# Edge lists sorted by matmul ranks, payload routed within sets and scattered in runs of four

## The chip, the cores and the metric

The kernel runs on one core of one Trainium2 chip. The metric is the device time of one execution in microseconds. The core has five engines with their own instruction queues: TensorE (PE), VectorE (DVE), ScalarE (ACT), GpSimd (POOL) and SyncE (SP). DMAs are issued from SP, ACT and POOL; indirect DMAs, which take a row number per partition from a column of a tile, only from POOL.

## The reference, cut

The program is two graph layers, each followed by a mixture of experts, on 6250 nodes of 256 features. Three edge lists appear in it: `src` for sums of edge attributes, `dst` (both 106250 edges) for two attention layers with one head, and `L1_ffn_edge_index[1]` (131072 edges) for an attention with four heads.

```python
time_feat = relu(edge_attr @ W_time.T + b_time)
sums = segment_sum(time_feat, src, num_segments=n)            # list 0
...
e = leaky_relu(el[src] + er[dst], 0.2)                        # list 1, twice
ex = exp(e - segment_max(e, dst, num_segments=n)[dst])
out = segment_sum(hp[src] * (ex / segment_sum(ex, dst)[dst])[:, None], dst)
...
agg = segment_sum(h[src] * alpha[:, :, None], dst, num_segments=M)   # list 2, four heads
```

## The kernel before

Nodes lie in 49 blocks of 128 (`NB`). Each list is sorted by node block: an edge's place in the sorted list is the start of its block plus its rank in the block, and blocks begin at multiples of a group of `KS[g]` x 128 edges, so that each group belongs to one block. `sorts` computes the places of the three lists one after the other on VectorE. The keys lie on 128 partitions in 832 (lists 0, 1) or 1024 (list 2) columns. For each block L368 counts its edges in a partition, TensorE sums the counts over partitions (L331), and then for each block L353 makes a mask, L354 a running count along the row and L358 copies the count into `posf` where the mask is set. List 0's places are made for the first `EARLY` columns and then for the rest, so that POOL may begin: for each of 832 columns it scatters 128 attribute rows of 33 numbers into `attr_sorted` (L274). SP loads these rows in chunks of 16 columns (`chunk`), each when a chunk four earlier has landed. ScalarE writes the node's place in the rows (L322). X (6.4 MB) is loaded near the beginning, and VectorE ends `sorts` with the statistics of X.

For lists 1 and 2 VectorE writes a payload of four words per edge (`pay`: the other node, the node's number in its block, and its bits as bytes, L409 to L415). POOL scatters it to `pay_sorted` column by column, 128 rows of 16 bytes an instruction (`scatter_pool`, L436): 832 and 1024 instructions, dealt out by hand over the stages that follow (the `scatter=` arguments in `program`). A stage is a block of its own: it ends when all engines are through with it, its scatters included.

The stages in order are sorts, edge_sums, norm_T, adapter, ln_stats, norm_T, router0, gates, experts, ln_stats, twice gat_tables and attention, finish, ln_stats, norm_T, router_tables, attention with four heads, and last_experts. The two attentions read `pay_sorted` in 16 parts (`PART` groups each) and POOL gathers a table row per edge, 128 per instruction (L770): 464 groups of 2 gathers for list 1, 304 groups of 4 for list 2. `NGS` holds the numbers of groups.

## Time and profile before

| | us |
|---|---|
| median of 3 runs | 8061.0 (8035.8 to 8073.2) |
| the profiled execution | 8044.4 |
| its span | 8042.6 |
| POOL busy | 5679.7 (71%) |
| VectorE busy | 5366.6 (67%) |
| TensorE busy | 4395.7 (55%) |
| ScalarE busy | 3591.1 (45%) |
| DMA, mean | 53 GB/s, 427 MB |

POOL's busy time doesn't hold the issue time between two of its DMAs, which the profile shows as idle time ended by "issue". The profile's chain of waits covers only the last stage (from 7825 us on), so the order of the stages before is read from the timeline of each engine.

### The profile page before, as it was taken

The page shows a single profiled execution, that of the slowest core. Times are in us where ns is not written, and L with a number is a line of the kernel's source. Part 1 is how long each engine was busy: PE and PEld are TensorE (multiplying, and loading weights), DVE is VectorE, ACT ScalarE, POOL GpSimd, SP SyncE. Part 2 cuts the span into 40 slices and gives each one's busy share as a digit, 9 for nine tenths or more (in the row PEclk, how much of TensorE's full clock was granted, in tenths as well). Part 3 has the DMA queues.
Part 4 walks back from the last instruction along what each step waited for, and adds up shares of the span by engine and source line. Part 5 has one row for each costly group of instructions (what it writes and reads, how often), then busy time and mean ns, then how long its engine had stood idle before and what let it go on. Part 6 is the DMA issues. An engine that isn't in the chain of part 4 may idle for free. (4 is left out here: it accounts for less than half of the span.)

```text
span 8042.6 us, 111241 instructions
## 1 busy us (share of the span) xinstructions
PE 4395.7 (55%) x22490; PEld 2790.5 (35%) x22610; DVE 5366.6 (67%) x18776; ACT 3591.1 (45%) x11436; POOL 5679.7 (71%) x5781
## 2 busy tenths in 40 slices
PE   0000007914269993566666656666612777777768
PEld 0000006912135552344444434444411344444435
DVE  9999407913212223677777767777741999999987
ACT  0000003411112221477777457777710788888862
POOL 2777777777677777777777777777766777777750
PEclk9999999956689996799999889999956899999989
DMA  6111111200010000244434234433301111111113
GB/s 162 26 24 26 24 24 41 52 4 3 3 29 2 2 2 14 76 107 108 108 107 107 71 91 108 108 107 107 107 10 29 23 27 28 27 27 28 27 32 118
DMA packets 476333, 427.34 MB, mean 53 GB/s; under 512 B 269726, under 2 KB 409876, under 8 KB 475668
## 3 DMA queue, kind: packets, MB, share of 16 engines
q0 software_dynamic: 214016, 282.62, 15.3%
q1 hardware_dynamic: 224020, 120.13, 5.6%
q10 hardware_dynamic: 37632, 17.48, 1.0%
q8 instruction: 203, 3.33, 0.2%
q14 instruction: 462, 3.78, 0.2%
HBM read 341.50 MB, written 78.72 MB: 52 GB/s over the span
## 5 line engine op out<-in xcount | busy, mean ns | idle before, releaser
L436 POOL DMA_INDIRECT pay_sorted<-pay,pos x1856 | 1889.8, 1018 | 697.8 <-issue 572.1
L770 POOL DMA_INDIRECT G<-tab_gat,pay x1856 | 1789.6, 964 | 592.4 <-issue 557.5
L770 POOL DMA_INDIRECT G<-tab_rt,pay x1216 | 1154.9, 950 | 433.8 <-issue 298.5
L274 POOL DMA_INDIRECT attr_sorted<-rows,pos x832 | 842.8, 1013 | 389.5 <-issue 253.3
L844 PE MATMUL pU<-G,PM 128*128 128x257 f32 x3712 | 1001.9, 394 | 1.1 <-DVE acc L1157 1.0
L790 PE MATMUL pA<-identb,G 128*20 128x128 bf16 (+1 forms) x3072 | 389.6, 226 | 933.9 <-DMA G<-tab_gat,pay 813.3
L889 ACT ACTIVATE aT<-pA 20x256 bf16<-20x256 bf16 (+1 forms) x1232 | 520.2, 422 | 517.2 <-PE pA L790 508.6
L1060 DVE TENSOR_REDUCE mt<-pW 128x4 f32<-128x2048 f32 x304 | 694.1, 2283 | 15.2 <-PE pW L808 13.8
L844 PEld LDWEIGHTS pU<-G,PM 128*128 128x128 f32 x3712 | 658.3, 198 | 58.1 <-ACT PM L941 1.2
L790 PEld LDWEIGHTS pA<-identb,G 128*20 128x20 bf16 (+1 forms) x3072 | 164.1, 92 | 1444.5 <-DMA G<-tab_gat,pay 1181.4
L322 ACT ACTIVATE rows<-lo 128x16 f32<-128x16 f32 x52 | 11.6, 229 | 1140.0 <-DMA attr_sorted<-rows,pos 1080.3
L935 ACT ACTIVATE e<-pW,adst 128x256 f32<-128x256 f32 x928 | 432.7, 466 | 165.4 <-DVE mt L1033 116.5
L1033 DVE TENSOR_REDUCE mt<-pW 128x1 f32<-128x256 f32 x928 | 389.7, 420 | 140.3 <-PE pW L800 126.6
L1649 DVE TENSOR_TENSOR t<-pO,BL 128x1024 f32<-128x1024 f32 (+1 forms) x78 | 90.7, 1163 | 580.4 <-PE pO L1601 580.3
L1633 ACT ACTIVATE H<-pH,B 128x512 f32<-128x512 f32 (+1 forms) x312 | 206.6, 663 | 591.0 <-PE pH L1590 590.1
L950 ACT ACTIVATE PT<-e,bias 128x256 f32<-128x256 f32 x928 | 456.8, 492 | 0.6 <-DVE e L1149 0.5
L1157 DVE SCALAR_TENSOR_TENSOR acc<-acc,alpha,pU 128x257 f32 x928 | 440.9, 475 | 7.8 <-PE pU L844 6.9
L1149 DVE SCALAR_TENSOR_TENSOR e<-e 128x256 f32<-128x256 f32 x928 | 398.0, 429 | 37.1 <-ACT e L935 2.7
L916 ACT ACTIVATE Nm<-iota,pay 128x128 bf16<-128x128 f32 x1216 | 383.2, 385 | 0.0
L816 PE MATMUL pP<-ident,PT 128*128 128x128 f32 x1856 | 369.6, 282 | 0.0
L335 PE MATMUL turned<-ident,gsum 128*1 128x128 f32 x24 | 5.6, 411 | 628.7 <-DVE gsum L404 628.7
L941 ACT ACTIVATE PM<-pP 128x256 f32<-128x256 f32 x928 | 334.2, 360 | 10.3 <-PE pP L816 9.1
(325 smaller groups left out, 11388.4 us busy)
## 6 DMA issues: line engine op xcount, KB each, us to landing
pay_sorted<-pay,pos POOLq DMA_INDIRECT x1856, 2.1
G<-tab_gat,pay POOLq DMA_INDIRECT x1856
G<-tab_rt,pay POOLq DMA_INDIRECT x1216, 2.4
expert_parts<-pos SPq DMA_DIRECT2D x144, 128.0 KB, 1.7
yl<-expert_parts SPq DMA_DIRECT2D x36, 512.0 KB, 3.8
attr_sorted<-zattr SPq DMA_DIRECT2D x1, 16896.0 KB, 53.5
rows<-attr_sorted ACTq DMA_DIRECT2D x256, 66.0 KB
attr_sorted<-rows,pos POOLq DMA_INDIRECT x832, 2.2
```

Of the source, the lines that this page charges most:

```text
L274: pool.indirect_dma_start(out=self.attr_sorted, out_offset=bass.IndirectOffsetOnAxis(ap=pos0[:, t:t + 1], axis=0), in_=rows[:, j, k, :], i ...
L436: pool.indirect_dma_start(out=out, out_offset=bass.IndirectOffsetOnAxis(ap=self.pos[g][:, lo + n:lo + n + 1], axis=0), in_=self.pay[g][:, ...
L770: pool.indirect_dma_start(out=G[:, j, k, 0:R], out_offset=None, in_=table, in_offset=bass.IndirectOffsetOnAxis(ap=pay[:, g % (2 * PART), k ...
L790: ins = nc.tensor.transpose(pA[j % len(pA)][:, k * P:(k + 1) * P], parts[:, k, 0:ROWS], self.identb[:, :])
L844: ins = nc.tensor.matmul(u[:, 0:F], PM[:, j % 2, k * P:(k + 1) * P], G[:, j, k, 0:F], start=(k == 0), stop=(k == K - 1))
L889: a.activation(aT[0:ROWS, j % 2, :], pA[j % len(pA)][:, 0:K * P], ACT.Copy).then_inc(s_aT, 1)
L935: a.activation(e[:, j % 2, :], pW[j % 2][:, 0:K * P], ACT.Identity, bias=ad).then_inc(s_y, 1)
L950: a.activation(PT[:, s, :], e[:, s, :], ACT.Exp, bias=bias[:, j % 4:j % 4 + 1]).then_inc(s_PT, 1)
L1033: v.tensor_reduce(mt, pW[s][:, 0:K * P], AX.X, ALU.max).then_inc(s_max, 1)
L1060: v.tensor_reduce(mt, pW[:, :, :], AX.X, ALU.max).then_inc(s_max, 1)
L1149: v.scalar_tensor_tensor(e[:, j % 2, :], e[:, j % 2, :], SLOPE, e[:, j % 2, :], ALU.mult, ALU.max).then_inc(s_e, 1)
L1157: v.scalar_tensor_tensor(ac, ac, alpha[:, j, 0:1], pU[j % 2][:, 0:F], ALU.mult, ALU.add).then_inc(s_acc, 1)
```

## The change

Ranks. VectorE only makes the masks (four buffers in turn). TensorE counts them by products with a column of ones, 128 columns of the list at a time, and sums ranks in PSUM by three kinds of products: the mask with a lower triangle (edges of earlier partitions), the counts of earlier columns, and the start of the block. VectorE copies the sums by the mask. `EARLY` goes from 208 to 256.

Payload. Lists 1 and 2 are cut into sets of 64 columns (13 and 16 sets). Within a set edges are sorted by block, each block rounded up to four edges (`CH`), into 128 x 17 chunks of four. Each half set of 32 columns is routed by 32 products: R is one-hot in the target partition, V holds three values (two parts of the other node's number, and the node's number) one-hot in the target column. R, Q and V are made by VectorE (tensor_tensor on bf16) in X's memory, so X is loaded after the last routing product. The sums of two half sets are kept (`keep`), and the payload words are built from them. `destinations` works out each chunk's row in `pay_sorted` (POOL's index), whose rows are now four edges, 64 bytes. POOL scatters 13 x 17 + 16 x 17 = 493 columns of chunks, within edge_sums, the first norm_T, the adapter and experts.

Around it. `NGS[1]` goes from 464 to 470 and `NGS[2]` from 304 to 309, since every block is rounded up in every set. The attention with one head reads `pay_sorted` as "(s p k)", that with four heads still as "(p s k)". Some small tiles of the last stages lie in the payload's memory.

```diff
 AR = 4
-EARLY = 208
...
+SC = 64
+CH = 4
+SETS = (None, ET // SC, FT // SC)
+MC = 17
+SLOTS = MC * CH
+NGS = (NG0,) + tuple((e + NB * (CH - 1) * n + NB * (k * P - CH)) // (k * P) for e, k, n in zip((E0, E1), KS[1:], SETS[1:]))
...
-        self.pay = [None, kp("pay1", [P, ET, PW], I32), kp("pay2", [P, FT, PW], I32)]
+        self.pos = [None] + [kp(f"pos{g}", [P, n], I32) for g, n in ((1, 4 * NB * NX1), (2, FT))]
...
         self.attr_sorted = nc.dram_tensor("attr_sorted", (NG0 * GE, ED + 1), F32).ap()
...
+        self.pay_sorted = [None] + [nc.dram_tensor(f"pay_sorted{g}", (NGS[g] * KS[g] * P // CH, CH * PW), I32).ap()
+                                    for g in (1, 2)]
         self.tab_gat = nc.dram_tensor("tab_gat", (PADROW + PADS, D + 3), F32).ap()
...
+            T8, HT = 8, 32
...
+            spare = self.X[:, 0:NB - 1, :].rearrange("p b d -> p (b d)").bitcast(BF16)
+            RN, VN = HT * P, 3 * SLOTS * HT
+            R = [spare[:, n * RN:(n + 1) * RN].rearrange("p (a r b) -> p a r b", a=HT // T8, b=T8) for n in range(2)]
+            V = [spare[:, 2 * RN + n * VN:2 * RN + (n + 1) * VN].rearrange("p (w a c b) -> p w a c b", w=3, a=HT // T8, b=T8)
+                 for n in range(2)]
+            Q = spare[:, 2 * RN + 2 * VN:2 * RN + 2 * VN + VN // 3].rearrange("p (a c b) -> p a c b", a=HT // T8, b=T8)
...
+            HALVES = (0, SETS[1] * SC // HT, FT // HT)
...
+                sp.wait_ge(s_routed, HALVES[1] + HALVES[2])
+                filled += self.load_x(sp)
...
+                def counts(g):
+                    for b in range(NB):
+                        n = masks[0]
+                        pe.wait_ge(s_mask, n + 1)
+                        for j in range(pairs(g)):
+                            ins = t.matmul(ptot[:, j * NB + b:j * NB + b + 1], mask[n % 4][:, j * P:(j + 1) * P], onesb[:, 0:1],
+                                           start=True, stop=True)
+                        ins.then_inc(s_used, 1)
+                        masks[0] += 1
...
+                def ranks(g, lo, to):
+                    for b in range(NB):
+                        n, u = masks[0], sels[0]
+                        pe.wait_ge(s_mask, n + 1)
+                        if u >= 2:
+                            pe.wait_ge(s_sel, u - 1)
+                        r = rank[u % 2]
+                        for a in range(lo, to, 512):
+                            z = min(a + 512, to)
+                            t.matmul(r[:, a - lo:z - lo], tris[0][:, :], mask[n % 4][:, a:z], start=True, stop=False)
+                        for a in range(lo, to, P):
+                            z = min(a + P, to)
+                            t.matmul(r[:, a - lo:z - lo], tot[:, a // P, b:b + 1].to_broadcast([P, P]), tris[min(g, 1)][:, 0:z - a],
+                                     start=False, stop=False)
+                        for a in range(lo, to, 512):
+                            z = min(a + 512, to)
+                            ins = t.matmul(r[:, a - lo:z - lo], off[0:96, b:b + 1].to_broadcast([96, P]), places_of(g)[0:96, a:z],
+                                           start=False, stop=True)
+                        ins.then_inc(s_used, 1)
+                        masks[0] += 1
+                        sels[0] += 1
...
+                def route(g):
+                    for h in range(HALVES[g]):
+                        n = halves[0]
+                        s, first_set = h // 2, HALVES[1] // 2 * (g - 1)
+                        pe.wait_ge(s_rv, n + 1)
+                        if h % 2 == 0 and first_set + s >= 2:
+                            pe.wait_ge(s_kept, first_set + s - 1)
+                        for k in range(HT):
+                            ins = t.matmul(routed[(first_set + s) % 2][:, 0:3 * SLOTS].rearrange("p (w c) -> p w c", w=3),
+                                           R[n % 2][:, k // T8, :, k % T8], V[n % 2][:, :, k // T8, :, k % T8],
+                                           start=(h % 2 == 0 and k == 0), stop=(h % 2 == 1 and k == HT - 1))
+                        ins.then_inc(s_routed, 1)
+                        halves[0] += 1
...
+                def make_mask(lo, to, b):
+                    n = masks[0]
+                    if n >= 4:
+                        dve.wait_ge(s_used, n - 3)
+                    v.tensor_scalar(mask[n % 4][:, lo:to], hi[:, lo:to], self.iota[:, b:b + 1], None, ALU.is_equal).then_inc(s_mask, 1)
+                    masks[0] += 1
...
-                        c(v.tensor_scalar(mm, hh, self.iota[:, b:b + 1], None, ALU.is_equal))
-                        c(v.tensor_tensor_scan(rk, mm, none[:, lo:hi_], base[:, b:b + 1], ALU.add, ALU.add))
-                        if keep:
-                            v.tensor_scalar(base[:, b:b + 1], rank[:, hi_ - 1:hi_], 0.0, None, ALU.add)
-                        c(v.copy_predicated(posf[:, lo:hi_], mm.bitcast(U16), rk))
...
+                def ranks(g, lo, to):
+                    def select(b):
+                        dve.wait_ge(s_used, first_mask + b + 1)
+                        v.copy_predicated(posf[:, lo:to], mask[(first_mask + b) % 4][:, lo:to].bitcast(U16), rank[sels[0] % 2][:, 0:to - lo])\
+                            .then_inc(s_sel, 1)
+                        sels[0] += 1
+                        dve.wait_ge(s_sel, sels[0])
+                    first_mask = masks[0]
+                    make_mask(lo, to, 0)
+                    for b in range(NB):
+                        if b + 1 < NB:
+                            make_mask(lo, to, b + 1)
+                        select(b)
...
+                def destinations(g):
+                    dve.wait_ge(s_iota, 5)
+                    dve.wait_ge(s_rep, g)
+                    n = SETS[g]
+                    for q in range(0, n, 5):
+                        w = min(5, n - q)
+                        both = rank[q // 10][:, q // 5 % 2 * 512:q // 5 % 2 * 512 + w * 2 * (NB + 1)]\
+                            .rearrange("p (s q b) -> p s q b", q=2, b=NB + 1)
+                        c(v.tensor_tensor(below[:, 0:w, :, :], chunk[:, :].unsqueeze(1).unsqueeze(3).to_broadcast([P, w, MC, NB + 1]),
+                                          both[:, :, 0, :].unsqueeze(2).to_broadcast([P, w, MC, NB + 1]), ALU.is_ge))
+                        c(v.tensor_tensor(below[:, 0:w, :, :], below[:, 0:w, :, :],
+                                          both[:, :, 1, :].unsqueeze(2).to_broadcast([P, w, MC, NB + 1]), ALU.mult))
+                        c(v.tensor_reduce(dsum[:, q:q + w, :], below[:, 0:w, :, :], AX.X, ALU.add))
+                    dve.sem_inc(s_repd, 1)
+                    to = self.pos[g][:, 0:n * MC]
+                    c(v.tensor_tensor(to.rearrange("p (s m) -> p s m", m=MC), dsum[:, 0:n, :],
...
+                def route(g):
+                    w, n_sets = width(g), SETS[g]
+                    kk = key[:, g, 0:w]
+                    src = key[:, 0, 0:w] if g == 1 else oth[:, :]
+                    m2, m3, f = mi[:, 0:w], mj[:, 0:w], posf[:, 0:w]
+                    c(v.tensor_copy(m2, f))
+                    c(v.tensor_scalar(m3, m2, 2, P - 1, ALU.logical_shift_right, ALU.bitwise_and))
+                    c(v.tensor_copy(rb[:, 0:w], m3))
+                    c(v.tensor_scalar(m3, m2, 9, 2, ALU.logical_shift_right, ALU.logical_shift_left))
+                    c(v.tensor_scalar(m2, m2, CH - 1, None, ALU.bitwise_and))
+                    c(v.tensor_tensor(cb[:, 0:w], m2, m3, ALU.add))
...
+                    def keep(s):
+                        first_set = HALVES[1] // 2 * (g - 1)
+                        dve.wait_ge(s_routed, HALVES[1] * (g - 1) + 2 * s + 2)
+                        v.tensor_copy(stage[:, s, :, :].rearrange("p w c -> p (w c)"), routed[(first_set + s) % 2][:, 0:3 * SLOTS])\
+                            .then_inc(s_kept, 1)
+                    for h in range(HALVES[g]):
+                        n = halves[0]
+                        if n >= 2:
+                            dve.wait_ge(s_routed, n - 1)
+                        def over(x, wide):
+                            return x[:, h * HT:(h + 1) * HT].rearrange("p (a b) -> p a b", b=T8).unsqueeze(2)\
+                                .to_broadcast([P, HT // T8, wide, T8])
+                        v.tensor_tensor(R[n % 2][:, :, :, :], places_r[:, :, :].unsqueeze(1).to_broadcast([P, HT // T8, P, T8]),
+                                        over(rb, P), ALU.is_equal)
+                        c(v.tensor_tensor(Q[:, :, :, :], places_c[:, :, :].unsqueeze(1).to_broadcast([P, HT // T8, SLOTS, T8]),
+                                          over(cb, SLOTS), ALU.is_equal))
+                        for q in range(3):
+                            ins = v.tensor_tensor(V[n % 2][:, q, :, :, :], Q[:, :, :, :], over(vals[:, q, :], SLOTS), ALU.mult)
+                        c(ins)
+                        dve.sem_inc(s_rv, 1)
+                        halves[0] += 1
+                        if h % 2 == 0 and h:
+                            keep(h // 2 - 1)
+                    keep(n_sets - 1)
...
-        PART = NG // 16
-        pay = sb("pay", [P, 2 * PART, K, PW], I32)
+        PART = -(-NG // 16)
+        if one:
+            pay = sb("pay", [P, 2 * PART, K, PW], I32)
+        else:
+            spare = self.pay[1][:, :, :].rearrange("p a b -> p (a b)")[:, 4 * K * P:4 * K * P + 2 * PART * K * PW]
...
+            rows = self.pay_sorted[gi].rearrange("n (e c) -> (n e) c", c=PW)
+            of = rows.rearrange("(s p k) c -> p s k c" if one else "(p s k) c -> p s k c", p=P, k=K)
             def load(part):
                 n = part % 2
-                sp.dma_start(pay[:, n * PART:(n + 1) * PART, :, :], of[:, part * PART:(part + 1) * PART, :, :]).then_inc(s_ld[n], 16)
+                w = min(PART, NG - part * PART)
+                sp.dma_start(pay[:, n * PART:n * PART + w, :, :], of[:, part * PART:part * PART + w, :, :]).then_inc(s_ld[n], 16)
...
-            k.edge_sums(acc0, scatter=[(1, 0, 384)])
+            k.edge_sums(acc0, scatter=[(1, 0, SETS[1] * MC), (2, 0, 60)])
             with nc.sbuf_tensor("XT0", [P, KT, NB * P], F32) as XT:
-                k.norm_T(XT, scatter=[(1, 384, 440)])
-                k.adapter(XT, acc0, scatter=[(1, 440, 588)])
-        k.ln_stats(scatter=[(1, 588, 612)])
+                k.norm_T(XT, scatter=[(2, 60, 76)])
+                k.adapter(XT, acc0, scatter=[(2, 76, 150)])
+        k.ln_stats(scatter=[])
         with nc.sbuf_tensor("XT1", [P, KT, NB * P], F32) as XT, nc.sbuf_tensor("LG0", [P, NB, NX0], F32) as LG, \
                 nc.sbuf_tensor("g0", [P, NB, NX0], F32) as g:
-            k.norm_T(XT, scatter=[(1, 612, 668)])
-            k.router0(XT, LG, scatter=[(1, 668, 724)])
-            k.gates(LG, g, NX0, True, scatter=[(1, 724, 738)])
+            k.norm_T(XT, scatter=[])
+            k.router0(XT, LG, scatter=[])
+            k.gates(LG, g, NX0, True, scatter=[])
...
                               (i["L0_ffn_expert_w2"], i["L0_ffn_expert_b2"], ACT.Relu),
-                              (i["L0_ffn_expert_w3"], i["L0_ffn_expert_b3"])], NX0, scatter=[(1, 738, ET), (2, 0, 560)])
...
-                k.gat_tables(layer, acc, m, adst, scatter=[(2, 584 + 104 * layer, 688 + 104 * layer)])
+                k.gat_tables(layer, acc, m, adst, scatter=[])
```

## Rows read from the trace of the kernel before

**Rows 1.** The page, costliest groups: count | busy, mean ns | idle before, releasers.

```profile
L436 POOL DMA_INDIRECT pay_sorted<-pay,pos x1856 | 1889.8, 1018 | 697.8 <-issue 572.1
L770 POOL DMA_INDIRECT G<-tab_gat,pay x1856 | 1789.6, 964 | 592.4 <-issue 557.5
```

**Rows 2.** Busy time by stretch; x counts instructions; last: granted clock, DMA share, GB/s.

```profile
1249.00:1769.00 520.00, 366.02 (x2816) 348.53 (x2816) 364.14 (x1795) 177.05 (x512) 391.95 (x384) 0.87 0.18 37
...
3318.70:4511.50 1192.80, 763.52 (x4177) 489.29 (x4177) 937.42 (x3751) 862.06 (x3250) 894.86 (x928) 0.97 0.40 106
...
6215.20:7797.00 1581.80, 1156.29 (x6717) 633.78 (x6838) 1468.85 (x6343) 1266.88 (x3710) 1154.95 (x1216) 0.94 0.17 29
```

**Rows 3.** POOL's timeline: start, us, instruction, in brackets idle time and its releaser.

```profile
140.24 1.14 POOL L274 DMA_INDIRECT attr_sorted<-rows,pos  x1 [136.21 <-DVE pos L388]
...
1234.10 0.97 POOL L274 DMA_INDIRECT attr_sorted<-rows,pos  x1 [0.31 <-issue]
1235.38 0.97 POOL L274 DMA_INDIRECT attr_sorted<-rows,pos  x1 [0.30 <-issue]
...
1761.54 0.97 POOL L436 DMA_INDIRECT pay_sorted<-pay,pos  x1 [0.30 <-issue]
```

**Rows 4.** VectorE's timeline, first instruction of a stage; in brackets the idle time.

```profile
1769.47 2.72 DVE L1242 TENSOR_SCALAR xn<-X,mean,rstd 128x256 f32<-128x256 f32 x8 [139.52 <-PEq L126]
...
1848.23 0.20 DVE L1313 TENSOR_SCALAR rc<-acc 128x49 f32<-128x49 f32 x1 [60.92 <-PEq L126]
...
2057.45 15.78 DVE L449 BATCH_NORM_STATS2 st<-X 128x6 f32<-128x256 f32 x48 [34.02 <-PEq L126]
...
2092.57 2.71 DVE L1242 TENSOR_SCALAR xn<-X,mean,rstd 128x256 f32<-128x256 f32 x8 [16.46 <-PEq L126]
...
2250.06 0.17 DVE L1498 TENSOR_SCALAR r<-iota 128x6 f32<-128x6 f32 x1 [27.26 <-PEq L126]
...
3133.56 15.78 DVE L449 BATCH_NORM_STATS2 st<-X 128x6 f32<-128x256 f32 x48 [74.53 <-PEq L126]
...
3318.72 0.15 DVE L996 CAST rown<-rowid 128x1 int32<-128x1 f32 x1 [33.98 <-PEq L126]
...
5859.12 0.47 DVE L1833 RECIPROCAL rd<-acc 128x49 f32<-128x49 f32 x1 [2.04 <-PEq L126]
...
5982.66 15.78 DVE L449 BATCH_NORM_STATS2 st<-X 128x6 f32<-128x256 f32 x48 [87.65 <-PEq L126]
...
6215.20 0.15 DVE L996 CAST rown<-rowid 128x1 int32<-128x1 f32 x1 [56.96 <-PEq L126]
```

**Rows 5.** Groups by shape, VectorE in sorts, list 2.

```profile
L354 DVE TENSOR_TENSOR_SCAN rank<-mask,base,none 128x1024 f32<-128x1024 bf16 x49 | 115.4, 2354 | 1.8
L358 DVE COPY_PREDICATED posf<-mask,rank 128x1024 f32<-128x1024 uint16 x49 | 63.2, 1291 | 1.7
L353 DVE TENSOR_SCALAR mask<-hi,iota 128x1024 bf16<-128x1024 bf16 x49 | 24.1, 491 | 1.7
```

**Rows 6.** Timelines of VectorE and POOL in experts and in finish.

```profile
2333.92 1.67 DVE L1656 SCALAR_TENSOR_TENSOR X<-t,g,X 128x256 f32<-128x256 f32 x4
...
2334.18 1.07 POOL L436 DMA_INDIRECT pay_sorted<-pay,pos  x1 [0.31 <-issue]
...
5865.49 17.12 POOL L436 DMA_INDIRECT pay_sorted<-pay,pos  x1 [0.30 <-issue]
...
5881.79 13.22 DVE L1845 TENSOR_TENSOR X<-X,acc 128x12544 f32<-128x12544 f32 x1
...
5882.91 12.96 POOL L436 DMA_INDIRECT pay_sorted<-pay,pos  x1 [0.30 <-issue]
```

**Rows 7.** Weight loads of TensorE in the attention with four heads.

```profile
6802.91 0.18 PEld L847 LDWEIGHTS pLU<-pfs,pay 128*128 128x128 bf16 x4
```

**Rows 8.** DMA issues: count, KB each, median us to landing.

```profile
tab_rt<-rows SPq DMA_DIRECT2D x1, 735.0 KB, 17.5
...
B<-in_L_ffn_expert_b_dram SPq DMA_DIRECT2D x2, 6.0 KB, 5.4
```

326 lines of the change are left out of this document (240 added, 86 removed).

## The prediction

> **What bounds the kernel now.** I read the costliest groups first [rows 1]: three kinds of indirect DMA on GpSimd (POOL) lead the list, and their idle time is almost all "issue", the engine's own 0.30 us between two of them. Next the stretches by stage [rows 2]: in edge_sums no compute engine fills its 520 us, and in the first attention POOL issues 928 gathers in 1193 us. Then POOL's own timeline [rows 3]: from 140 us on it issues one indirect DMA per 1.278 us (1234.10 to 1235.38) with nothing but stage boundaries between. Last, VectorE's first instruction of each stage [rows 4]: the bracket is the time since its last one of the stage before, in which only scatters were running. Where no scatter stands in front of a boundary (the start of finish, 5859.12) that is 2.04 us. So POOL's queue sets the end from 140 us to the start of the last stage, and each scatter removed is worth its 1.28 us until the stage's compute becomes the longer.
>
> **What is removed.** 1856 payload scatters become 13x17 + 16x17 = 493 (sets times MC). They now stand in edge_sums (281), the first norm_T (16), the adapter (74) and experts (122); the other stages have none. Stage by stage, against the compute that is left:
>
> edge_sums: 384 scatters filled the stage from its start at 1249 to 1762.5 [rows 2, 3], 1.337 us each; 281 take 375 us, with the 7 us from the last issue to the next stage (1762.5 to 1769.47) and a wait between the two lists of about 3 us that is 386 us. VectorE's end, 139.5 us before 1769.47, lies 381 us after the start, so POOL still ends it, by little: 520 - 386 = 134 us saved. First norm_T: 78.8 us from 1769.47 to 1848.23; 16 scatters and the 7 us leave 28, saved 51. Adapter: 34.0 - 2 = 32 [rows 4]. Three ln_stats: 16.46 - 2 = 14.4 each, 43 (the other two are alike). Two further norm_T: 60.9 less 2 for the last transposes and copies (an estimate) and 2 for the boundary, 57 each, 114. router0: 27.3 - 2 = 25; gates some 8 (an estimate: 14 scatters and a tail against its own chain). experts: 74.5 - 2 = 72. Two gat_tables: 34.0 - 2 = 32, and some 28 for the second, which is alike. finish: 87.65 - 2 = 86. router_tables: 57.0, of which the store of its table keeps 17 (17.5 us to landing [rows 8], issued 2.5 us before VectorE ends, then the boundary): 40. Sum: 666 us.
>
> **What is added outside the sorts.** Rounding each node block up to four edges per set makes more groups: NGS goes from 464 to 470 and from 304 to 309. Two layers of 6 groups of 2 gathers, 24 x 1.265 us (busy plus issue over 1856 [rows 1]) = 30 us. The router's attention takes 1581.8 us for 304 groups [rows 2], 5.2 each: 5 groups, 26 us. In attention for one head the payload is now read as "(s p k)", 3840 pieces of 32 bytes per part in place of 128 long ones. The nearest row is a bias load that I count as 1536 pieces of 4 bytes and that lands in 5.4 us [rows 8]; in proportion 13.5 us, against some 2 now (an estimate). Later parts are asked for 14 groups ahead (36 us), so only the first load of each layer shows: 2 x 11 = 22 us; bounds 0 and 50. Together 78 us. A scatter row of 64 bytes in place of 16 I cost at nothing: gathers of about 1 KB issue at the same 0.96 us [rows 1].
>
> **The sorts.** They end with POOL, not with VectorE: first scatter 140.24, last 1235.38, 832 x 1.278 = 1063 us of issue and 33 us lost. Three things move.
>
> (a) The start. VectorE's steps to the first 256 columns: preamble to 9.7 us (about 30 small operations instead of four), key split 1.3, 49 count masks, 0.49 us at 1024 columns [rows 5] so about 0.46 at 896, each waiting for seven TensorE products; four weight loads of bf16 take 0.18 us [rows 7], so seven take 0.3 and I allow 0.55 per block, 27 us. Base chain 6, lo0 and fill 2, then 49 rank steps of mask and predicated copy. The scan, 2.354 us at 1024 columns, is gone [rows 5]; at 256 columns mask and copy are about 0.3 + 0.43 and a hand-over to TensorE, 0.85 us, 42 us. Sum 89, so POOL starts 51 us earlier (bounds 75 and 115).
>
> (b) VectorE's own end. Ranks for 1024 columns cost 0.49 + 1.29 + 0.1 = 1.9 us per block instead of 4.2; TensorE's 12 products there carry 3072 columns, about 1.3 us at 2.4 GHz and 2.6 at 1.2, so either way near VectorE's pace. My sum: list 0 done at 158, list 1's ranks, chunk destinations and value preparation at 332, its routing 195, its words 27, list 2's ranks at 748, routing 240, words 31: about 1020 us. The load of X, now behind the routing, is issued when chunk 47 of 52 has been scattered, 84 us before POOL ends; load and statistics (some 60 us) fit under it. So VectorE doesn't set the end unless it loses 200 us more.
>
> (c) The routing blocks POOL. This is the term that decides. The one-hot tables R, Q and V are made by tensor_tensor with both inputs in SBUF. The row X<-X,acc in finish is such an operation, 13.22 us long, and the scatter issued under it took 12.96 us instead of 0.97 [rows 6]: it waited for the operation's end. Shorter ones let it in between: under a burst of four (1.67 us) a scatter took 1.07, it got in at the next instruction [rows 6]. The Trainium skill (SBUF — State Buffer, SBUF: two separate sides) has a VectorE operation with two SBUF inputs hold a port pair for its whole length against a GpSimd operation that reads SBUF; the first pair of rows agrees, and by its word alone scatters pass only between instructions.
>
> Length of one half set: R has 4096 elements, Q and the three of V 2176 each. The f32 row gives 1.054 ns an element (13.22 us over 12544). No row has two bf16 inputs; the bound below is the bf16 mask, 0.27 ns a column. I take half the f32 price, since all operands are bf16 in runs of 8: 2.3 + 4 x 1.3 = 7.5 us, and 14.5 at the full price. (The Trainium skill, VectorE: DVE Perf Modes, tier table, gives tensor_tensor 1224 ns for 2048 bf16 elements against 2293 in f32; by it a half set is an estimate of 7.6 us. No row here shows it.) In a half set there are five ends of instructions, two of them followed by a wait. With one scatter per boundary and 1.278 us between two, four pass per half set: POOL loses 58 x (7.5 - 4 x 1.278) = 139 us. Bounds: five or more pass and nothing is lost; only the two waits let one through, 58 x (7.5 - 2.56) = 287.
>
> About 10 us more go to the new integer preparation. The sorts change by -51 + 139 + 10 = +98 us.
>
> **Sum.** The profiled execution took 8044.4 us (span 8042.6), 17 below the median of 8061. 8044 - 666 + 78 + 98 = 7554; I say 7555.
>
> **The rivals.** (1) Nothing is blocked by bf16 pairs: 7555 - 139 = 7416. For it: only f32 rows show blocking. Against it: what blocks looks like the second input, not the type. (2) Scatters pass only at waits: 7555 + 148 = 7703. For it: in finish a scatter issued into 45 short operations without waits waited until the last, 17.12 us [rows 6]. Against: the burst row, whose four operations are nearest to the two and three of a half set. (3) tensor_tensor runs at the f32 price: 14.5 us per half set, five pass, 58 x (14.5 - 6.4) = 470 lost, VectorE ends near 1430 and POOL still after it: 7555 + 331 = 7886. (4) The 32-byte pieces slow the gathers: if the attention's 1.27 us rose by a tenth, 2 x 119 more, 7793; against it, the DMA engines are busy 0.40 there [rows 2]. (5) Slower than before: f32 price and one scatter per half set, so that POOL loses 58 x (14.5 - 1.28) = 767 us: 7555 + 628 = 8183. It turns slower once a half set costs POOL more than 10.8 us beyond what it issues. (6) The change doesn't do what it says: the stages keep their length without scatters. Against it, rows 4 leave no other releaser.
>
> **How the numbers follow.** Forecast 0.54, (1) 0.12, (2) 0.15, (3) 0.08, (4) 0.05, (5) and (6) 0.04, the rest spread. The range 7400 to 7800 holds forecast, (1), (2) and (4) with 30 us either way for my stage estimates; (3), (5) and (6) lie outside. About 0.5% is what this kernel's measurement can tell from no change. Faster by over 0.5%: 0.94; within it 0.03; slower 0.03.
>
> **What would show it.** edge_sums near 386 us with POOL last; VectorE's brackets at about 2 us before experts, finish and the rest; first scatter near 89 us; attr scatters of 2 us and more in the routing, four to a half set; tensor_tensor of 4096 bf16 elements at 2.3 us; sorts over at about 1345 us; 940 gathers in each of the two attention layers at 1.27 us. I am wrong if VectorE, not POOL, ends the sorts, if the attention slows by its payload loads, or if the half set is twice as long.

## The result and the profile after

The kernel after takes 7510.5 us (median of 4 runs, 7502.3 to 7522.8) against 8057.2 for the kernel before (4 runs): a ratio of 0.9327, 95% interval 0.9306 to 0.9347. The forecast of 7555 was 0.6% high. The profiled execution took 7504.9 us with a span of 7503.1, so the span shrank by 539.5 us, where the prediction's terms sum to 490.

First the ends of the stages. These are VectorE's first instructions of each stage in its timeline of the kernel after; the columns are those of [rows 4]: start, us, instruction, and in brackets the idle time before it with its releaser.

```profile
1332.27 0.27 DVE L833 MEMSET wt<- 128x256 f32 x1 [55.77 <-PEq L133]
1719.11 2.08 DVE L1553 TENSOR_SCALAR xn<-X,mean,rstd 128x256 f32<-128x256 f32 x6 [3.50 <-PEq L133]
1743.61 0.20 DVE L1624 TENSOR_SCALAR rc<-acc 128x49 f32<-128x49 f32 x1 [7.24 <-DVEq L133]
1921.77 15.78 DVE L754 BATCH_NORM_STATS2 st<-X 128x6 f32<-128x256 f32 x48 [1.23 <-PEq L133]
1941.13 2.03 DVE L1553 TENSOR_SCALAR xn<-X,mean,rstd 128x256 f32<-128x256 f32 x6 [0.70 <-PEq L133]
2817.63 2.71 DVE L754 BATCH_NORM_STATS2 st<-X 128x6 f32<-128x256 f32 x8 [1.06 <-PEq L133]
2953.64 0.15 DVE L1307 CAST rown<-rowid 128x1 int32<-128x1 f32 x1 [3.43 <-PEq L133]
5498.74 0.47 DVE L2144 RECIPROCAL rd<-acc 128x49 f32<-128x49 f32 x1 [1.74 <-PEq L133]
5535.12 15.78 DVE L754 BATCH_NORM_STATS2 st<-X 128x6 f32<-128x256 f32 x48 [0.70 <-PEq L133]
5654.25 0.15 DVE L1307 CAST rown<-rowid 128x1 int32<-128x1 f32 x1 [15.24 <-PEq L133]
```

The brackets that were 16 to 140 us in [rows 4] are now 0.7 to 7 us, but for the 15.24 us ahead of the last attention, where the table's store is waited for, and the 55.77 us at the end of the sorts, where POOL still runs. The differences of neighbouring rows are the stage lengths, set beside those of [rows 4]. The sorts of the kernel before end with this row of the same timeline:

```profile
1248.79 0.27 DVE L528 MEMSET wt<- 128x256 f32 x1 [90.74 <-PEq L126]
```

| from, to | before | after | change | predicted |
|---|---|---|---|---|
| sorts (to the first instruction of edge_sums) | 1248.8 | 1332.3 | +83.5 | +98 |
| edge_sums | 520.7 | 386.8 | -133.9 | -134 |
| first norm_T | 78.8 | 24.5 | -54.3 | -51 |
| adapter | 209.2 | 178.2 | -31.0 | -32 |
| first ln_stats | 35.1 | 19.4 | -15.7 | -14 |
| norm_T to experts | 1041.0 | 876.5 | -164.5 | -162 |
| ln_stats and gat_tables | 185.2 | 136.0 | -49.2 | -46 |
| two attentions, the gat_tables between | 2540.4 | 2545.1 | +4.7 | +24 |
| finish | 123.5 | 36.4 | -87.1 | -86 |
| ln_stats to router_tables | 232.5 | 119.1 | -113.4 | -111 |
| last attention and last_experts | 1827.4 | 1848.9 | +21.5 | +26 |

Second the sorts. The page of the kernel after, costliest groups: count | busy, mean ns | idle before, releasers.

```profile
L1081 POOL DMA_INDIRECT G<-tab_gat,pay x1880 | 1807.5, 961 | 1484.1 <-DMA pay<-pay_sorted 912.0
L340 POOL DMA_INDIRECT attr_sorted<-rows,pos x832 | 983.2, 1182 | 328.1 <-issue 252.8
L463 PE MATMUL routed<-X 128*128 128x204 bf16 x1856 | 681.4, 548 | 117.1 <-DVEq L669 117.1
L741 POOL DMA_INDIRECT pay_sorted<-pay,pos x493 | 503.3, 1021 | 367.5 <-POOLq L133 190.5
```

The payload scatters (L741) are 493 in place of the 1856 of [rows 1], at the same mean, 1.02 us, though their rows are four times as long. The attribute scatters (L340) have a mean of 1.18 us where their unhindered length is 0.97. The idle time of L1081 that is put down to a payload load is mostly POOL idling in the stages before: the two first gathers have brackets of 768 and 144 us, which begin at the last scatter of experts and at the last gather of the first layer.

Where the scatters lose their time is read from the busy time by stretch. Columns as in [rows 2]; the fifth pair is POOL's busy time and its scatters. The stretches are: up to the routing of list 1, that routing, list 1's payload words, the masks that count list 2, the routing of list 2, its words.

```profile
82.70:311.60 228.90, 136.04 (x1376) 80.33 (x1374) 207.57 (x318) 2.31 (x10) 177.10 (x171) 0.80 0.22 37
311.60:608.70 297.10, 289.64 (x790) 115.06 (x791) 192.04 (x142) 2.78 (x12) 238.00 (x195) 0.50 0.12 22
608.70:655.00 46.30, 15.83 (x44) 6.01 (x42) 29.68 (x23) 0.46 (x2) 38.38 (x27) 0.50 0.12 21
655.00:676.00 21.00, 18.19 (x392) 14.23 (x392) 20.47 (x51) 0.00 (x0) 19.78 (x5) 0.50 0.02 6
841.00:1208.00 367.00, 359.90 (x981) 142.88 (x982) 235.84 (x175) 3.50 (x15) 294.80 (x237) 0.50 0.12 22
1208.00:1257.70 49.70, 16.00 (x44) 6.08 (x42) 33.10 (x23) 1.51 (x2) 42.26 (x25) 0.50 0.47 142
```

A stretch's length less 1.278 us for each scatter is what POOL lost: 10.4, 47.9, 11.8, 14.6, 64.1 and 17.8 us. The routing accounts for 112 us of it, the words and the masks for 44. In all, from the first scatter at 82.73 to the last at 1318.11, 832 scatters lost 173 us, against 33 in [rows 3].

What one half set looks like: VectorE's timeline and then POOL's, in the routing of list 1.

```profile
448.47 2.29 DVE L662 TENSOR_TENSOR X<-iotar,rb 128x4096 bf16<-128x4096 bf16 x1 [4.23 <-PE routed L463]
450.68 1.28 DVE L664 TENSOR_TENSOR X<-iotac,cb 128x2176 bf16<-128x2176 bf16 x1
452.00 3.79 DVE L667 TENSOR_TENSOR X<-X,vals 128x2176 bf16<-128x2176 bf16 x3
460.20 0.37 DVE L650 COPY stage<-routed 128x204 f32<-128x204 f32 x1 [4.42 <-PE routed L463]
...
449.22 2.38 POOL L340 DMA_INDIRECT attr_sorted<-rows,pos  x1 [0.30 <-issue]
451.91 0.97 POOL L340 DMA_INDIRECT attr_sorted<-rows,pos  x1 [0.30 <-issue]
453.19 0.97 POOL L340 DMA_INDIRECT attr_sorted<-rows,pos  x1 [0.30 <-issue]
...
659.33 16.32 POOL L340 DMA_INDIRECT attr_sorted<-rows,pos  x1 [0.30 <-issue]
```

R takes 2.29 us, Q 1.28, the three of V 3.79: the half price in bf16 that the prediction took. (The Trainium skill, VectorE: DVE Perf Modes, tier table, from which an estimate of 7.6 us per half set was made: the trace agrees, 2.29 + 1.28 + 3.79 = 7.4 us.) But then VectorE waits 4.2 to 4.4 us for TensorE, and a half set takes 11.5 us (297.1 / 26 = 11.4 and 367 / 32 = 11.5), not 7.5. A scatter issued under R (449.22) ends at 451.60, 0.84 us after R (450.76). In VectorE's wait the scatters go through at their own pace, so that 7.4 to 7.5 pass per half set, not four. The last row is the scatter that was issued under the 49 masks that count list 2: it took 16.3 us.

### The profile page after: what moved, and what is told of

Same layout as the page of the kernel before. It is cut to its first block and busy times, and to the rows that moved or that the text cites. A ratio compares the mean times of both kernels' runs of the same rounds, so it can differ in the third digit from the quotient of the medians.

```text
span 7503.1 us, 121197 instructions
## 1 busy us (share of the span) xinstructions
PE 5403.8 (72%) x27581; PEld 3244.1 (43%) x27581; DVE 5507.1 (73%) x19032; ACT 3618.6 (48%) x11575; POOL 4472.6 (60%) x4467
## 5 line engine op out<-in xcount | busy, mean ns | idle before, releaser
L1081 POOL DMA_INDIRECT G<-tab_gat,pay x1880 | 1807.5, 961 | 1484.1 <-DMA pay<-pay_sorted 912.0
L1081 POOL DMA_INDIRECT G<-tab_rt,pay x1236 | 1172.4, 949 | 598.5 <-issue 301.2
L340 POOL DMA_INDIRECT attr_sorted<-rows,pos x832 | 983.2, 1182 | 328.1 <-issue 252.8
L463 PE MATMUL routed<-X 128*128 128x204 bf16 x1856 | 681.4, 548 | 117.1 <-DVEq L669 117.1
L741 POOL DMA_INDIRECT pay_sorted<-pay,pos x493 | 503.3, 1021 | 367.5 <-POOLq L133 190.5
L390 ACT ACTIVATE rows<-lo 128x16 f32<-128x16 f32 x52 | 11.7, 231 | 1204.7 <-DMA attr_sorted<-rows,pos 1170.6
L463 PEld LDWEIGHTS routed<-X 128*128 128x128 bf16 x1856 | 270.0, 146 | 527.5 <-issue 409.8
```

The costliest lines, as they stand in the source:

```text
L340: pool.indirect_dma_start(out=self.attr_sorted, out_offset=bass.IndirectOffsetOnAxis(ap=pos0[:, t:t + 1], axis=0), in_=rows[:, j, k, :], i ...
L463: ins = t.matmul(routed[(first_set + s) % 2][:, 0:3 * SLOTS].rearrange("p (w c) -> p w c", w=3), R[n % 2][:, k // T8, :, k % T8], V[n % 2] ...
L741: pool.indirect_dma_start(out=out, out_offset=bass.IndirectOffsetOnAxis(ap=self.pos[g][:, lo + n:lo + n + 1], axis=0), in_=self.pay[g][:, ...
L1081: pool.indirect_dma_start(out=G[:, j, k, 0:R], out_offset=None, in_=table, in_offset=bass.IndirectOffsetOnAxis(ap=pay[:, g % (2 * PART), k ...
```

## The experiments

Each kernel here was run once, but for the last two (four runs each). Four runs of the kernel after lie within 20 us, so what a smaller difference means is read from the timelines and not from the spans.

**Stages alone.** The kernel before with fewer payload scatters.

```diff
-            k.edge_sums(acc0, scatter=[(1, 0, 384)])
+            k.edge_sums(acc0, scatter=[(1, 0, 281)])
...
-                k.norm_T(XT, scatter=[(1, 384, 440)])
-                k.adapter(XT, acc0, scatter=[(1, 440, 588)])
-        k.ln_stats(scatter=[(1, 588, 612)])
+                k.norm_T(XT, scatter=[(1, 281, 297)])
+                k.adapter(XT, acc0, scatter=[(1, 297, 371)])
+        k.ln_stats(scatter=[])
```

> The kernel before, with 493 of its 1856 payload scatters, in the stages and numbers of the kernel after (281 in edge_sums, 16 in the first norm_T, 74 in the adapter, 122 in experts); the other 1363 columns are left unsorted, so most gathers read rows of empty places. Sorts and attention stay as they were. Theory: each stage was held by the scatters in front of its boundary, and they are worth what the stages lost between the two traces: from 520.7 + 78.8 + 244.3 + 88.5 + 68.9 + 62.0 + 862.1 + 144.5 + 148.9 + 158.6 + 88.4 + 109.1 us to 386.8 + 24.5 + 197.5 + 30.8 + 46.9 + 50.8 + 773.3 + 110.7 + 119.0 + 55.7 + 31.1 + 68.7, 679 us in all: span 8042.6 - 679 = 7364, or 7377 by the 666 of the prediction. Rival: part of these 679 us comes from other things in the change (scatter rows of 64 bytes in place of 16, another order of loads), then less is saved here: 7450 and more.

The span was 7357.9, 684.7 us less than before, against 679 expected. (The 679 hold the gat_tables between the two attentions, 148.9 to 119.0, which the table above has in the row of the attentions.) So the stages' gain comes from the number of scatters. The 6 us more are within the spread. The longer rows cost nothing that shows: from the start of edge_sums to the start of the first attention this run, with rows of 16 bytes, took 1621.6 us (1246.12 to 2867.70), and the kernel after, with rows of 64, 1621.4 (1332.27 to 2953.64).

**The tables left out.** R, Q and V made for two half sets only.

```diff
+                        if n < 2:
-                        v.tensor_tensor(R[n % 2][:, :, :, :], ...
+                            v.tensor_tensor(R[n % 2][:, :, :, :], ...
```

> The one-hot tables R, Q and V are made for the first two half sets only; the other 56 half sets route with those tables (so the payload words are those of the first sets). All 1856 products, all copies and all scatters stay. Theory: the tensor_tensors with two SBUF inputs are what costs POOL 113 us in the two routing stretches (433 scatters in 664 us where 1.278 us each would be 553). Without them scatters go through at 1.278 us there: 113 us less lost, POOL's last scatter near 1206 us instead of 1319. VectorE's chain stays, since TensorE's 32 products of 0.367 us set the half set at 11.5 us: it ends near 1276 and takes over the end of the sorts, next stage at about 1290 instead of 1332, span 7503 - 43 = 7460. Rival: scatters are slowed in the routing by TensorE's reads or by the scatters' own DMA, not by VectorE: POOL's last scatter stays at 1319 and the span at 7503.

POOL's timeline, last attribute scatter and first payload scatter:

```profile
1188.39 0.97 POOL L340 DMA_INDIRECT attr_sorted<-rows,pos  x1 [0.30 <-issue]
1273.54 0.97 POOL L742 DMA_INDIRECT pay_sorted<-pay,pos  x1 [84.18 <-SPq L775]
```

The last scatter came at 1188 (1206 expected): 130 us earlier, the 112 of the routing and the 18 of list 2's words, which no scatter was left to meet. VectorE then ended the sorts, at 1270.3, and POOL's next stage began at 1273.5 (1290 expected); span 7439.1 (7460 expected). So VectorE's tables are what POOL loses to in the routing, and behind POOL stood VectorE, some 43 us earlier (1276.5 in the kernel after). The prediction had it some 300 us earlier.

**R twice.**

```diff
-                        v.tensor_tensor(R[n % 2][:, :, :, :], ..., over(rb, P), ALU.is_equal)
+                        for _ in range(2):
+                            c(v.tensor_tensor(R[n % 2][:, :, :, :], ..., over(rb, P), ALU.is_equal))
```

> R is made twice in each half set, each time with a wait for its own end. Theory: VectorE idles 4.4 us per half set for TensorE, so the half set stays at 11.5 us and VectorE's end at 1276; but a scatter that meets R waits for its end, and a second R of 2.29 us lets one scatter pass where 1.8 would: about 1.0 us lost each, 58 us in all. POOL's last scatter near 1377, next stage at 1390, span 7561. Rival one (the loss is not VectorE's): no change, 7503. Rival two (TensorE does not set the half set, VectorE does): half set 13.8 us, VectorE ends 58 x 2.3 = 133 us later at 1409 and the span is 7593.

The half sets kept their length (list 1's routing ended at 627 in place of 625), so TensorE does set it. But the last scatter came at 1439.81, 122 us later, 2.1 us per half set in place of 1.0, and the span was 7631.3 (7561 expected). My rule, one loss per long operation, was too simple: with R doubled a scatter also came too late for the end of a V and waited for a whole one (2.10 us in place of 0.97; 119 scatters of 1.9 to 2.15 us, 23 in the kernel after). What POOL loses depends on how its 1.278 us fall against the ends of VectorE's operations.

**What makes TensorE slow.** Products over neighbouring columns, and inner runs of two and of four.

```diff
-                                           R[n % 2][:, k // T8, :, k % T8], V[n % 2][:, :, k // T8, :, k % T8],
+                                           R[n % 2][:, :, :, :].rearrange("p a r b -> p (a r b)")[:, k * P:(k + 1) * P],
+                                           V[n % 2][:, :, :, :, :].rearrange("p w a c b -> p w (a c b)")[:, :, k * SLOTS:(k + 1) * SLOTS],
```

> The routing products read the same tables as runs of neighbouring columns, where the kernel reads every eighth column (16 bytes apart), and the routed values are multiplied by 0 in the copy out of PSUM: all payload words are those of empty places. Count and size of the products stay. Theory one (the step of 16 bytes makes a product take 0.367 us): a product falls to the 0.28 us that 128 + 204 columns take at 1.2 GHz, or to 0.14 at 2.4; the half set is then set by VectorE at 7.5 to 9 us, VectorE ends 58 x 2.5 to 4 us = 145 to 230 us earlier, and POOL, with fewer gaps to use, passes 4 to 5 scatters per half set: last scatter 1319 to 1345, span 7503 to 7530. Theory two (weight load and product follow each other at 1.2 GHz whatever the step): 0.367 us stays, nothing changes.

```diff
-            T8, HT = 8, 32
+            T8, HT = 2, 32
```

> The inner run of the tables (T8) is 2 elements in place of 8, so that the products read columns 4 bytes apart in place of 16; the result is the same. Theory one of the run before (the step is what costs TensorE): the product takes 0.28 us or less. Theory two: 0.367 us stays. On VectorE the runs of two may lift the price of the tables: unchanged, R at 2.29 us, or towards the f32 price, R at 4.3 us and the half set 14 us, set by VectorE; then POOL loses 5 passages fewer than 11 per half set, VectorE ends 58 x 2.5 = 145 us later and sets the end of the sorts: span 7503 + 100 = 7600. I take the unchanged price: span 7503 to 7530.

```diff
-            T8, HT = 8, 32
+            T8, HT = 4, 32
```

> The inner run of the tables (T8) is 4 elements, so that the routing products read columns 8 bytes apart; the result is the same. At 16 bytes a product took 0.367 us, at 4 bytes 32 of them took 2.9 to 4.8 us, 0.09 to 0.15 each. Theory one (a product's time grows with the step): between the two, by proportion 0.18 to 0.22 us, 32 in 5.8 to 7 us; VectorE still sets the half set at 7.7 us and the span is that of e5, 7500. Theory two (only steps of 16 bytes are slow): 32 in 2.9 to 4.8 us, span 7500 also. Theory three (any step over 4 bytes is as slow as 16): half set 11.7 us, span 7503 and VectorE's payload words done near 1258 us in place of 1010.

Spans: 7490.5, 7500.0 and 7492.0. TensorE's weight loads in the routing (start, us, instruction, count), first in the kernel after, one load per 0.37 us:

```profile
450.08 0.14 PEld L463 LDWEIGHTS routed<-X 128*128 128x128 bf16 x1 [0.22 <-issue]
450.45 0.14 PEld L463 LDWEIGHTS routed<-X 128*128 128x128 bf16 x1 [0.22 <-issue]
```

Then with runs of two, the 32 of a half set in 5.23 and in 2.87 us:

```profile
447.04 5.23 PEld L463 LDWEIGHTS routed<-X 128*128 128x128 bf16 x32 [3.40 <-DVEq L669]
454.43 2.87 PEld L463 LDWEIGHTS routed<-X 128*128 128x128 bf16 x32 [2.16 <-DVEq L669]
```

And with runs of four, 32 in 5.68 and in 5.66 us:

```profile
431.44 5.68 PEld L463 LDWEIGHTS routed<-X 128*128 128x128 bf16 x32 [2.00 <-DVEq L669]
454.03 5.66 PEld L463 LDWEIGHTS routed<-X 128*128 128x128 bf16 x32 [1.74 <-DVEq L669]
```

The granted clock was not the same in these half sets, and has to be read beside them. Busy time by stretch, columns as above (the third number from the end is the clock), two half sets with runs of two and then the two with runs of four:

```profile
447.10:452.10 5.00, 5.00 (x30) 4.33 (x31) 4.96 (x4) 0.00 (x0) 4.09 (x4) 0.50 0.04 8
454.50:457.20 2.70, 2.70 (x31) 2.70 (x32) 2.70 (x3) 0.00 (x0) 2.40 (x2) 1.00 0.49 79
431.50:437.00 5.50, 5.50 (x31) 3.74 (x32) 5.47 (x4) 0.00 (x0) 4.59 (x4) 0.50 0.04 9
454.10:459.60 5.50, 5.50 (x31) 3.65 (x32) 5.46 (x5) 0.00 (x0) 4.58 (x4) 0.69 0.31 51
```

At a granted clock of 0.50 a product takes 0.367 us with columns 16 bytes apart, 0.18 at 8 bytes and 0.16 at 4, so that the 32 of a half set take 11.7, 5.7 and 5.2 us. At 1.00 it takes 0.09 us with 4 bytes; with 8 bytes a half set that ran partly at 1.00 took as long as one at 0.50. VectorE's tables keep their price in all three (R 2.287 us in each). So the step was the cause: at the same clock 16 bytes take 2.2 times as long as 4, and the 5.2 us of 4 bytes are already less than VectorE's 7.5. The rest of the fall to 2.87 us is the clock. Of the three expectations for 8 bytes the last two fall, and the 5.7 us lie just under the range of the first. (The Trainium skill, Advanced Engine Details and Errata, Memory Cachelines, says that SBUF is read in lines of 16 bytes, that at least two hits on a line are needed to hide the access, and that a new line at every access is slower. The 0.367 us at 16 bytes agrees. Two hits per line, 8 bytes, come near four hits at 0.50, 5.68 against 5.23 us, but not once the clock rose, 5.66 against 2.87.)

Busy time by stretch with runs of two, where the half set is VectorE's:

```profile
312.00:505.00 193.00, 112.53 (x800) 95.56 (x800) 188.44 (x140) 1.85 (x8) 156.76 (x120) 0.74 0.11 21
752.00:970.00 218.00, 130.41 (x928) 110.82 (x928) 212.73 (x160) 1.84 (x8) 179.31 (x128) 0.76 0.11 20
```

VectorE is busy 188 of 193 us; the half set takes 7.7 us and its last payload words were done at 1010 us. These are the 7.5 us and the 1020 us of the prediction. Yet the last scatter came only 12 us earlier (1306.5): with no idle time on VectorE 4.6 scatters pass in a half set, and over the 447 us of both routings (the two rows are 411 of them) POOL loses 102 us, nearly the 112 of before. That is why products that are two to four times as fast buy almost nothing by themselves.

**In step.** The remaining question was what lets scatters through. In the timelines above a scatter that met an operation was through 0.84 us after its end, and 0.30 us later the next one was issued. So if VectorE's operations follow each other at 1.21 us (the three V), scatters at 1.278 slip back by 0.07 each time, until one comes too late and waits for a whole operation. Two edits on top of the runs of two: each V waits for its end (which adds 0.12 us), and R is made in two halves, each of which waits too.

```diff
-                            ins = v.tensor_tensor(V[n % 2][:, q, :, :, :], Q[:, :, :, :], over(vals[:, q, :], SLOTS), ALU.mult)
-                        c(ins)
+                            c(v.tensor_tensor(V[n % 2][:, q, :, :, :], Q[:, :, :, :], over(vals[:, q, :], SLOTS), ALU.mult))
...
+                        for a in range(2):
+                            z = HT // T8 // 2
+                            c(v.tensor_tensor(R[n % 2][:, a * z:(a + 1) * z, :, :],
+                                              places_r[:, :, :].unsqueeze(1).to_broadcast([P, z, P, T8]),
+                                              over(rb, P)[:, a * z:(a + 1) * z, :, :], ALU.is_equal))
```

The three runs are both edits, the waits of the V alone (R whole), and the halves alone (without waits).

> The kernel with runs of two (e5), and in the routing VectorE waits for the end of each of its operations, with R made in two halves. Theory: a scatter that meets a tensor_tensor waits for its end and goes through in 0.85 us after it; the next wants to issue 1.17 to 1.28 us after that end. Q and V (1.21 us from start to start) are a little shorter than that, so after two or three of them a scatter comes too late for the boundary and waits for a whole operation (2.09 us in place of 0.97), and it loses 0.9 us or more to R (2.21). A wait adds 0.12 us: 1.33 for Q and V, 1.27 for half an R, so that each of the six operations lets one scatter through. Half set 7.7 + 0.2 = 7.9 us, 6 scatters in place of 4.6: the loss in the routing falls from 102 us to 58 x (7.9 - 6 x 1.278) = 14, POOL's last scatter from 1306 to 1218, span 7500 - 88 = 7412. Rival (POOL is let in in proportion to VectorE's idle time, whatever the length of an operation): VectorE is as busy as before, about 4.7 per half set, no gain, 7500 or a little more.

> As e6, but R stays whole. Theory: operations of 2.21, 1.33 and three times 1.33 us, half set 7.7 us; five scatters pass, 58 x (7.7 - 5 x 1.278) = 76 us lost in place of 102: POOL's last scatter near 1280, span 7474. Rival: no gain, 7500.

> The kernel with runs of two (e5), R made in two halves of 1.15 us, without the added waits. Theory (a scatter wants to issue 1.17 to 1.28 us after the end that let it in, so operations that are a little shorter than this lose it a whole operation every time, and only longer ones are met in step): 4 to 5 scatters per half set, as with R whole; routing loses 100 us or more, span 7500 to 7520. Rival (more ends of operations are all that is needed): 5.5 to 6 per half set, as in e6, span near 7410.

Spans: 7402.5 (7412 expected), 7476.8 (7474) and 7535.6 (7500 to 7520). VectorE and then POOL of the run with both, in one half set:

```profile
457.08 2.48 DVE L664 TENSOR_TENSOR X<-iotar,rb 128x2048 bf16<-128x2048 bf16 x2
459.60 1.29 DVE L667 TENSOR_TENSOR X<-iotac,cb 128x2176 bf16<-128x2176 bf16 x1
460.93 3.94 DVE L670 TENSOR_TENSOR X<-X,vals 128x2176 bf16<-128x2176 bf16 x3
...
458.08 1.07 POOL L340 DMA_INDIRECT attr_sorted<-rows,pos  x1 [0.31 <-issue]
459.46 0.97 POOL L340 DMA_INDIRECT attr_sorted<-rows,pos  x1 [0.30 <-issue]
460.73 1.00 POOL L340 DMA_INDIRECT attr_sorted<-rows,pos  x1 [0.30 <-issue]
462.04 1.02 POOL L340 DMA_INDIRECT attr_sorted<-rows,pos  x1 [0.30 <-issue]
463.37 1.02 POOL L340 DMA_INDIRECT attr_sorted<-rows,pos  x1 [0.30 <-issue]
464.69 1.02 POOL L340 DMA_INDIRECT attr_sorted<-rows,pos  x1 [0.30 <-issue]
```

Six operations, 1.26 to 1.33 us from start to start, and six scatters of about 1.0 us, one at each end. The routing loses 25 us in place of 102, and the last scatter came at 1215.62 (1218 expected). With the waits alone five pass (80 us lost), with the halves alone 4.1 (144 us lost, 42 more than with R whole): more ends without the right spacing make it worse. How that goes, VectorE and then POOL of the run with the halves alone:

```profile
455.22 2.35 DVE L664 TENSOR_TENSOR X<-iotar,rb 128x2048 bf16<-128x2048 bf16 x2
457.49 1.29 DVE L667 TENSOR_TENSOR X<-iotac,cb 128x2176 bf16<-128x2176 bf16 x1
...
455.94 1.34 POOL L340 DMA_INDIRECT attr_sorted<-rows,pos  x1 [0.31 <-issue]
457.59 2.03 POOL L340 DMA_INDIRECT attr_sorted<-rows,pos  x1 [0.30 <-issue]
```

The second scatter began 0.02 us after the end of R (457.57) and waited for all of Q. The waits are not what lets scatters in: in these three runs all 664 scatters that began more than 0.15 us ahead of the end of such an operation ended 0.84 to 0.86 us after that end, also the 173 of them where VectorE went on without a wait. VectorE is nearly as busy with both edits as without (185.5 of the 193 us from 312 on, against 188.4; it ends its words 30 us later), and with the halves alone fewer scatters pass than with R whole, so its busy share does not decide.

**Start and masks.** On the runs of two: the first part of the ranks is 128 columns, and the masks that count list 2 wait for their own ends.

```diff
-EARLY = 256
+EARLY = 128
...
                         make_mask(0, w, b)
+                        if g == 2:
+                            dve.wait_ge(s_mask, masks[0])
```

> The kernel with runs of two (e5); the 49 masks that count list 2 (0.46 us each, one behind the other, under which one scatter took 16.3 us) each wait for their own end, and the first scatter waits for the ranks of 128 columns in place of 256. Theory: the scatters get through at these waits, 16 us less lost at about 600 us; 49 rank steps of 0.84 us become some 0.6, the first scatter starts 12 us earlier at 71 us (the fill of the target lands at about 57). POOL's last scatter 1306 - 16 - 12 = 1278, span 7472. Rival for the masks: the wait adds 49 x 0.1 us and POOL still gets in only at the end: no gain from them, span 7488.

The first scatter started at 70.08, and under the masks nothing was lost (14 us in the run without the waits). But the span was 7503.0, 31 us more than expected: in the routing 4.1 scatters passed per half set in place of 4.6, and 141 us were lost there in place of 102. The earlier start shifted the scatters against the operations and took back what the two edits gave.

**All together.** The run with both edits, the earlier start, the waits on the masks, and the casts of the payload words in halves; then with list 2's scatters all in experts.

```diff
-                        c(v.tensor_copy(bytes_[:, :, :, q], kk2))
+                        for a, z in ((0, n_sets // 2), (n_sets // 2, n_sets)):
+                            c(v.tensor_copy(bytes_[:, a:z, :, q], kk2[:, a:z, :]))
```

> e6 with the first scatter after the ranks of 128 columns, a wait behind each of the 49 masks that count list 2, and the casts of the payload's bits (2.35 us each) in two halves. Theory: start 12 us earlier, 3.6 us less lost under the masks (they lost that in e6), some 15 of the 30 us that the payload words still cost POOL: span 7402 - 31 = 7372, last scatter near 1185. Rival: the shift of the start moves the steps of scatters and operations against each other (as in e8) and takes some of it back: up to 7402.

```diff
-            k.edge_sums(acc0, scatter=[(1, 0, SETS[1] * MC), (2, 0, 60)])
+            k.edge_sums(acc0, scatter=[(1, 0, SETS[1] * MC)])
...
-                k.norm_T(XT, scatter=[(2, 60, 76)])
-                k.adapter(XT, acc0, scatter=[(2, 76, 150)])
+                k.norm_T(XT, scatter=[])
+                k.adapter(XT, acc0, scatter=[])
...
-                              (i["L0_ffn_expert_w3"], i["L0_ffn_expert_b3"])], NX0, scatter=[(2, 150, SETS[2] * MC)])
+                              (i["L0_ffn_expert_w3"], i["L0_ffn_expert_b3"])], NX0, scatter=[(2, 0, SETS[2] * MC)])
```

> e9 with all 272 scatters of list 2 in experts, none in edge_sums, the first norm_T and the adapter beyond list 1's 221 in edge_sums. Theory: edge_sums is then VectorE's (383 us of 387, so 3 us less), the first norm_T keeps its own 19 of 24.5 us, the adapter and experts are longer than their scatters: 8 to 10 us less than e9. Rival: 150 more scatters in experts meet its two-input operations and POOL's writes slow those: no gain or some us more.

The first took 7377.6 us (4 runs, 7369.1 to 7390.1; span 7372.4 as expected), 0.918 of the kernel before (0.916 to 0.920). Its last scatter came at 1186.30. The second took 7364.3 us (7354.3 to 7373.9), 0.916 (0.914 to 0.918); its span is 11.8 us below the first's (8 to 10 expected), 6.5 of it in edge_sums (390.0 to 383.5) and 4.1 in the first norm_T (24.3 to 20.2) by VectorE's first instructions, while the stages from the second norm_T to experts keep their 876 us with 150 scatters more. The two ranges overlap, so the second step is shown by the profile only. Their medians lie 133 and 146 us below that of the kernel after.

## Why the prediction was right, and where it was not

**Stages (-666 predicted).** Right in every row of the table, the largest miss being a little over 3 us. Reading a bracket in front of a stage boundary as the price of the scatters there holds, and the run with fewer scatters shows it by itself (684.7 us).

**Outside the sorts (+78).** The table's rows grew by 4.7 and 21.5 us, and the first of them holds the second gat_tables, 29.9 us shorter: 56 us in all, 22 less than forecast. The gathers are 1880 at 0.96 us, as priced. The term that was mis-sized is the payload load in pieces of 32 bytes, 11 us each: the two parts of 120 KB land in 4.8 us, and the first gather comes 4.2 us after the stage's first instruction (2953.64 to 2957.77) in place of 2.2 (3318.72 in [rows 4] to the first gather at 3320.95), 2 us each. A price per piece taken from a bias load of 4-byte pieces was too high. This term is 18 of the 22 us; the rest is a last attention that grew by 21.5 us in place of 26.

**Sorts (+98): the sum was right by two errors.** (a) The start: 82.73 in place of 89; the 49 rank steps take 0.84 us each, as priced to 1 us in all, so the other 5 lie ahead of them. (b) VectorE's own end: this step failed. Its last payload words were done at 1257.7 in place of 1020, and its statistics of X followed them, to 1276.5. I set TensorE's pace for the ranks from the count of columns and did not price the routing products at all; they read every eighth column, and 32 of them take 11.7 us where VectorE needs 7.5. With runs of two the 1020 came out as 1010. That it did not show in the time is luck: POOL still ended 43 us later. (c) The loss: 139 us predicted for the routing, 112 measured. VectorE's waits for TensorE, which I had not foreseen, let three more scatters through per half set; with VectorE busy throughout, as I had it, 4.6 pass and 102 us are lost (runs of two): nearly each of the five ends let one through, where I had four. The other 61 of the 173 us are the masks that count list 2 (15), the words (30), the 229 us before the routing (10) and what is left between; the kernel before lost 33 us over its sorts. So POOL lost 140 us more than before, where the prediction added 139 for the routing alone; that the two agree is luck, for the 140 come from several places. The sorts came out 14.5 us below the sum by the start (57 us earlier, not 51) and by the 10 us for integer work, which are already in these 140.

**The rivals.** (1), nothing blocked, falls with the scatter of 2.38 us under R. (2), passing at waits alone, falls for these operations: scatters pass at the end of R, where Q follows at once (449.22 above, and the 173 counted in the runs in step); for masks of 0.46 us it is nearer to the truth (16.3 us). (3) and (5) fall with R at 2.29 us, (4) with the gathers at 0.96 us and their issue, (6) with the table. (The Trainium skill, SBUF — State Buffer, SBUF: two separate sides, has a VectorE operation with two SBUF inputs block, for its whole length, a GpSimd operation that reads SBUF: R and V agree. By it an operation in a mode that uses two ports does so too; the masks, with one tensor input, held a scatter for 16.3 us, but no run here shows their mode.)

## What to carry to other kernels

Idle time in front of a stage boundary, read engine by engine, priced 1363 removed DMAs to 3 us a stage. A step in a TensorE operand has to be priced like an operation: here 16 bytes cost 2.2 times as much as 4 bytes at the same granted clock, and VectorE makes the tables at the same price for either. Where POOL issues indirect DMAs beside long VectorE operations, it is the spacing of their ends against POOL's own period that counts: a little above it almost nothing is lost, a little below it a whole operation each few times.

## What the runs showed of the hardware

The granted TensorE clock stood at 0.50, the level of 1.2 GHz, through both routing stretches of the kernel after, though the profile counts TensorE as busy for 97 to 98% of them. Ahead of it TensorE had been at 1.00 in list 1's ranks (to 260 us), at 0.50 in the few short products that follow them, and then without a product for 53 us; in list 2's ranks, from 700 to 770 us, it was at 1.00 again. Busy time by stretch of the kernel after, same columns as above:

```profile
220.00:240.00 20.00, 16.90 (x153) 9.09 (x150) 19.50 (x29) 0.23 (x1) 15.74 (x15) 1.00 0.14 26
280.00:300.00 20.00, 0.00 (x0) 0.00 (x0) 19.79 (x7) 0.23 (x1) 15.23 (x16) 0.50 0.14 25
```

With steps of 4 bytes the clock was 0.74 to 0.76 on average in the same work, changing between its two levels from one half set to the next, with TensorE busy 58 to 60%. So the busy share of the profile does not tell the clock. Whether 0.367 us would be less at 2.4 GHz no run shows; with 8 bytes the half set took 5.68 us at 0.50 and 5.66 at an average of 0.69.

What stays open is when a run of short masks lets a scatter in. Under the same 49 masks one scatter took 14.7 to 17.9 us in eight runs, but in the run with both edits none took more than 2.07 us and 12 began and passed there, without a wait between the masks: ten of them in a row at 1.58 us from start to start, which is four masks (0.396 us each from start to start). What made this one fall in step is not shown. With a wait behind each mask nothing was lost in the run on the start and the masks, nor in the first one of all together.
